# A macaron block on one core: the attention part routes twelve token tiles instead of fourteen, and the second expert part four instead of two

## What is computed

```python
x = x + 0.5 * ffn(layernorm(x))       # part f1
x = x + attention_block(layernorm(x)) # attention
x = x + 0.5 * ffn(layernorm(x))       # part f2, same weights as f1

def ffn(x):                           # E = 8 experts, K = 2 of them per token
    logits = silu(x @ rw1 + rb1) @ rw2 + rb2
    w = softmax over the two largest logits of a token
    return x + sum over those two experts e of w[e] * (silu(x @ we1[e] + be1[e]) @ we2[e] + be2[e])

def attention_block(x):               # 16 heads of 64, causal linear attention in 256 tokens
    x = x + linear_attention(layernorm(x)) @ Wo
    return x + gelu(layernorm(x) @ Wf1) @ Wf2
```

## Time and profile before

| | us |
|---|---|
| median of 3 runs | 2001.55 |
| lowest, highest | 1998.72, 2002.62 |
| profiled execution, its own time | 2005.34 |
| its span in the trace | 2003.6 |
| PE busy | 1698.4 (85%) |
| DVE busy | 1558.9 (78%) |
| ACT busy | 1072.6 (54%) |
| POOL busy | 968.9 (48%) |

### The profile page before, as it was taken

One profiled execution on the slowest core, in us unless ns is written; L12 is line 12 of the kernel. 1 busy time (PEld: TensorE's weight loads), 2 busy tenths in 40 slices (PEclk: granted clock), 3 DMA queues, 4 the chain that ended last, 5 costly groups with the idle time before them and its releaser, 6 DMA issues. The chain is left out here.

```text
span 2003.6 us, 36381 instructions
## 1 busy us (share of the span) xinstructions
PE 1698.4 (85%) x12527; PEld 1384.7 (69%) x12527; DVE 1558.9 (78%) x4234; ACT 1072.6 (54%) x1935; POOL 968.9 (48%) x1010
## 2 busy tenths in 40 slices
PE   4448799984999999999999999999999956799990
PEld 3236688863778777777777777777777745687770
DVE  7667687765888888988888888898888626577774
ACT  2125577753556556555565555655556424577770
POOL 4876401115544465555546546445553324566661
PEclk9998899996999999999999999999999967899995
DMA  7554677740000010000001001001000004577757
GB/s 228 190 179 132 227 254 263 264 156 13 12 9 9 9 20 18 11 19 19 12 16 20 16 12 21 18 9 20 17 12 12 12 11 180 201 235 249 231 195 266
DMA packets 91664, 190.31 MB, mean 95 GB/s; under 512 B 15021, under 2 KB 52570, under 8 KB 80474
## 3 DMA queue, kind: packets, MB, share of 16 engines
q1 hardware_dynamic: 45738, 131.26, 19.3%
q0 software_dynamic: 33840, 46.17, 8.7%
q10 hardware_dynamic: 11904, 10.55, 1.5%
HBM read 131.08 MB, written 56.85 MB: 94 GB/s over the span
## 5 line engine op out<-in xcount | busy, mean ns | idle before, releaser
L1551 POOL TENSOR_TENSOR at_sc<-at_sc 128x512 f32<-128x512 f32 x128 | 198.2, 1548 | 344.4 <-DVE at_sc L1651 344.1
L551 ACT ACTIVATE f_hid<-f_up_ps,f_w 128x512 f32<-128x512 f32 x312 | 214.3, 688 | 155.0 <-PE f_up_ps L426 126.3
L1643 DVE SCALAR_TENSOR_TENSOR at_qk<-at_exps,at_relus 128x512 f32<-128x512 f32 x256 | 182.8, 715 | 100.5 <-ACT at_relus L1460 97.9
L1651 DVE TENSOR_TENSOR at_sc<-at_s_ps,mask 128x384 f32<-128x384 f32 x512 | 251.7, 550 | 1.1 <-PE at_s_ps L1284 1.1
L892 DVE TENSOR_TENSOR f_hid_lo<-f_hid,f_hid_hi 128x512 fp32r<-128x512 f32 x312 | 209.2, 688 | 14.8 <-ACT f_hid_hi L558 3.1
L665 POOL DMA_INDIRECT expert_rows<-f_rows_out,f_dest x156 | 165.3, 1059 | 97.1 <-DVE f_rows_out L915 60.5
L1958 POOL DMA_INDIRECT x<-finished_rows,slot x120 | 195.7, 1631 | 29.7 <-issue 29.7
L1524 ACT ACTIVATE raw<-at_num_ps 128x512 f32<-128x512 f32 x128 | 76.1, 595 | 241.2 <-PE at_num_ps L1321 220.6
L648 POOL DMA_INDIRECT sent_rows<-f_xn,slot x144 | 148.8, 1034 | 69.5 <-issue 40.8
L1281 PE MATMUL at_s_ps<-at_qk 64*128 64x256 f32 x1024 | 172.0, 413 | 6.7 <-issue 4.3
L1459 ACT ACTIVATE at_exps<-at_proj_ps 128x512 f32<-128x512 f32 x253 | 152.4, 603 | 36.2 <-PE at_proj_ps L1259 29.4
(11 more groups left out here) (324 smaller groups left out, 4802.8 us busy)
## 6 DMA issues: line engine op xcount, KB each, us to landing
f_w<-split_weights SPq DMA_DIRECT2D x78, 1028.0 KB
f_got<-sent_rows SPq DMA_DIRECT2D x78, 264.0 KB, 4.7
finished_rows<-f_rows_out POOLq DMA_DIRECT2D x39, 256.0 KB, 2.5
split_weights<-f_split SPq DMA_DIRECT2D x8, 1024.0 KB
sent_rows<-f_pads SPq DMA_DIRECT2D x16, 264.0 KB
x<-in_L_attn_x SPq DMA_DIRECT2D x16, 256.0 KB, 5.1
raw<-in_L_ffn_we SPq DMA_DIRECT2D x16, 256.0 KB
out_x<-x ACTq DMA_DIRECT2D x16, 256.0 KB, 4.4
```

The source lines that it names most:

```text
L551: A(hid[:, c, :], up_bank(n)[:, :], ACT.Silu, bias=w[:, i % RING_W, 4 * HID + c:4 * HID + c + 1].bitcast(FP32)).then_inc(s_silu, 1)
L1551: g.tensor_tensor(sc[:, n % RING_SC, :, 3, :], sc[:, n % RING_SC, :, 1, :], sc[:, n % RING_SC, :, 2, :], ALU.add).then_inc(s_sum, 1)
L1643: stt(full, exps[:, p % 2, :], 1.0, relus[:, p % 2, :], ALU.min, ALU.add).then_inc(s_phi, 1)
L1651: last = tt(flat(sc[:, (n // 2) % RING_SC, 2 * (n % 2) + half, 0:3, :]), s_ps[2 * (n % 2) + half][:, 0:3 * P], flat(mask[:, :, :]), ALU.mult)
```

## The change

Two numbers of `macaron_kernel`:

```diff
-        k.routed = k.tiles - 2
+        k.routed = k.tiles - 4
         spent = ffn_phase(nc, k, "f1", start=0, begin=9, join=11, x_in=tile_in, loads=loads)
         attention_phase(nc, k, spent)
-        ffn_phase(nc, k, "f2", start=k.routed, begin=k.routed, join=k.tiles - 1, out=tile_out)
+        ffn_phase(nc, k, "f2", start=k.routed, begin=k.routed, join=k.tiles - 3, out=tile_out)
```

## The result

The changed kernel is slower: median 2016.81 us (2007.84 to 2026.50, 5 runs) against 2001.15 (1997.25 to 2002.62, 5 runs), ratio 1.008, 95% interval 1.0043 to 1.0118. The forecast was 2002.5 with a range to 2010. The profiled execution is its fastest one, span 2006.1; it also had an f1 8.6 us shorter than the one before, in code that is the same in both. So the two spans can't be subtracted. The stages can.

What follows compares the result with a forecast made beforehand. Attention was taken as bound by PE (93% busy) and its waits, f2 by waits between tiles. f2's +11.57 less attention's 10.55 gave +1.0 us on 2005.34, a median of 2002.5, with an 8-in-10 range of 1993 to 2010.

Steps and rivals of the forecast that it cites:

- the terms of the rounds: Attention, rounds 26 to 30: each routing step removed gives back its share of the round's length, compared with round 2.
- a sign of being wrong: Attention: rounds 29 and 30 staying at 34 us and more would mean DVE or ACT set the round, not routing.
- The tail: Attention, round 32: without the 8 sends ahead of it, the root of norm C starts 3.72 us earlier, counted whole.
- The last interval at 12.10 and the one before it at 13.53: f2 before T: three intervals taken from f1, 8.23, 13.53 and 12.10, together 33.86 against 7.13, so T comes 26.73 later.
- 1.9 back: f2 behind T: longer iterations let queues empty, returning a quarter of the 7.8 us by which f1 resumes sooner.
- The first result goes back behind 32 sends and not 16: f2, POOL: eight sends take 10.1 us, less than an interval of 12 to 13.5, so no cost was counted.
- the edit costed at nothing: f2, POOL: first result behind 32 sends, not 16; if POOL fell 4 to 6 us behind, the wait behind the pads covers it.
- starved sends: Rival, f2: DVE's fast-mode copies delay POOL's sends, some 24 us more, 2026; chance 0.04.
- the pads at f1's pace: Rival, f2 behind T: 7.8 us back and not 1.9, net -4.9, 1996.7; chance 0.12.
- no stalls: Rival, f2: iterations don't stall, intervals 8.23, 9.21 and 7.78, net -7.6, 1994; chance 0.18.
- the slower one: Rival, f2: stalled intervals 15.23 and 13.53, pads as slow as before, net +6.1, 2007.6; chance 0.28.

## Why the prediction was wrong

**Attention** was 14.3 us less, forecast 10.55. The direction and the places held, the terms of the rounds did not. Round by round the forecast was 0.1, 1.41, 0.96, 2.40, 1.96 and 0 for 26 to 31, and the profile has 0.8, 0.37, 2.14, 1.10, 2.54 and 1.12 less: the terms were off one by one, the sum (8.1 against 6.83) less so. That the sum came near is luck: rounds 27 and 29 gave back far less than forecast (29 took 34.29 us, and the prediction had named 34 and more as a sign of being wrong), 28, 30 and 31 more. Another 1.0 lies in the rounds up to 25, where nothing is changed. The tail gave 5.2 and not 3.72. The root's own term was right: it starts 3.72 us behind its input before and 0.07 after, 3.65 less. Of the rest 1.3 lies ahead of that input (22.71 and 21.40 us from the last denominators to it); no run shows why. The clock was no part of it (0.99 in both).

**f2** was 25.4 us more, forecast 11.57. This is where it failed, in three steps (the first two are 14.8 us; the lone tiles gave 1.0 more back than forecast):
- The last interval at 12.10 and the one before it at 13.53, both from f1: they were 10.63 and 20.29. Sum of the three 39.21 against 33.86.
- "1.9 back" behind T: instead 5.5 more (39.87 for 34.33), and 2.1 more to the next tile. This is the largest miss, 9.5 us.
- "The first result goes back behind 32 sends and not 16 ... POOL is as far at T as before": with the sends it was (11 were left at T, before 13). But the results of four expert tiles run without a break behind them, before those of one: 24 indirect DMAs in one run, 1700.6 to 1731.3, where before it was a run of 20, 1681.9 to 1708.9. Tile 7 comes 3.8 us behind its end; before, tile 5 came 11.5 behind it.

The step behind all three is the edit costed at nothing: I asked whether POOL would be late with the sends, and found that it wasn't. What counts is that POOL's unbroken run makes the others late. Sends after T make the intervals short (8.29, 8.67, 7.55), breaks of 1 us make intervals and stretch short with as many sends, 8 more lengthen an interval by 10 us. Each alone could be read otherwise (the 8 more are also more traffic), but together they leave the unbroken run: it went with the stall each time, while the number of sends, their traffic and the iteration's work stayed. It was to be seen before: f1's long intervals, with their "remote" waits, went with breaks in f1, and the 22.32 us of the pads beside the run of 20 fell to 8.80 in the kernel before with breaks in f2. I had taken the one for the nature of an iteration and left the other open.

The rule of the Trainium skill that I weighed (SBUF — State Buffer, the box "The 'DVE blocks DMA' trap (SWDGE)") names the same engine but another victim: sends starved by DVE. Here the sends of the changed kernel (least, median, most ns) show none of it, and DVE had 2.11 us of work in the 9 of the stall; the row of ACT above is what is late.

```profile
L648 POOL DMA_INDIRECT sent_rows<-f_xn,slot x160: 954/959/1796, 28.4 to 1709.6; - x160
```

The rival "starved sends" didn't happen. Of the others, "the pads at f1's pace" and "no stalls" didn't either; the slower one had the right sign and place, but with 15.23 for the long interval and the pads as before (+6.1 us net) it was too mild.

Open is what in the chip holds the signals back. The runs show when it happens, and the trace that it is the semaphore's step that comes late, but not by what path; in the 9 us of the stall there was neither a weight load nor much traffic.

## To carry to other kernels

Indirect DMAs on POOL aren't paid only on POOL: look for the long runs of them in the timeline, and for waits without a cause beside them, before moving more of them into one place. Break the runs (1 us behind 4 was enough here, 0.2 us wasn't), but count what POOL then takes for a tile, for if it falls behind, it catches up in a run and the stall comes back later. An interval copied from another stage of a kernel carries that stage's stalls; ask what makes it long before it goes into a sum.

## What the runs showed of the hardware

- Beside a run of indirect DMAs on POOL, semaphore steps of other engines come late: by 7 to 11 us in a run of 16 (PE's for ACT, at 1682.12 to 1682.37). ACT's wait was 9.5 us there and 20.4 in a run of 48. The last such wait ends about when the run does, from 3 us ahead of its end to 11 behind it.
- The first 8 or so of a run (10 us) harm nobody as far as the rows show: 8 pads were issued in 9.20 us beside the first of 48, against 22.32 in the kernel before.
- The last lone tiles, where POOL has runs of 4 with 1.4 us or more between, take 6.5 to 6.6 us each (median of the last 15) in every kernel.
- A break may be an operation of 1.0 to 1.6 us or POOL standing idle for 2 us; an addition of 0.21 us isn't one.
- f1, the same code in 14 of the profiles, took 507.2 to 529.1 us to the first denominators.
